# TensorE's order of scores, weighted sums and work-bank tasks in a fused attention kernel

## The chip, the core and the metric

The kernel runs on one core of a Trainium2 chip. The metric is the device time of one execution in microseconds (us); before the change it is 2196.08 us, the median of three runs (2194.22 to 2198.04).

## What is computed

The input x has 16 sequences of 512 tokens with 256 channels. An attention layer with two sets of keys and values comes first, then a gated recurrence over the 16 sequences as steps. The attention part, which the change concerns, is per sequence:

```python
q = heads(x @ Wq)                                   # 16 heads of 16 channels
out_short = softmax(q @ k_s.T / 4 + decay_bias) @ v_s   # decay_bias[i, j] = -|i - j| * (1 - decay)
out_long  = softmax(q @ k_l.T / 4) @ v_l
out = (alpha * out_short + (1 - alpha) * out_long) @ Wo
x = layernorm(x + out)
```

Behind it, for the recurrence: c = f * c + i * g with three gates from x and c, h = tanh(x Wo' + c Uo' + b), and a second layernorm(x + h).

## The kernel before, in words

**Units and slots.** For every sequence b (a batch) there are UNITS = 8 units. A unit is four heads of one of the two attentions: even units are the long one, odd ones the short one with its bias. A unit has TC = 4 slots, one for each chunk of 128 keys, so a batch has 32 slots. Scores are computed twice. `scores(b, s, hp)` makes them with the keys on the partitions, for the exponential (kind "b" below), and `scores_for_max(b, s, hp)` with the queries on the partitions, for the row maxima of the unit that is AHEAD = 8 slots further (kind "a"). Each call makes two heads (hp is 0 or 1), one in each half of the array's rows, and fills one pair of PSUM banks with 128 x 1024 numbers. In odd units `bias` and `bias_for_max` add small bf16 products on the diagonal blocks (`diagonals`) and only then is the pair full.

**Three pairs of banks.** The 16 fills of a unit go round PAIRS = 3 pairs of banks in the order of the list FILLS (line 107). `banks_free` (line 605) makes TensorE wait for the reader of the fill three places earlier in that list: ScalarE's exponential for a "b" fill, VectorE's reduction for an "a" fill. In this text b11 means kind "b", slot 1 of the unit, hp 1, and so on.

**The other work on TensorE.** `weigh_before` (line 673) is the weighted sum of the slot before, probabilities by values, in eight matmuls of 32 columns each side by side; it waits for both exponentials of that slot. `work_task` (line 718) is one task of the list TASKS in a single work bank: "kq" projects keys or queries of the next batch, in two halves, "v" projects values, "ot" turns the attention output, "wo" is the output projection, and "turn" (slot 1 of every unit) turns the unit's weighted sums and the next unit's maxima. `work_free` waits until the readers of the task before are done. A turn waits for ScalarE's copy of the weighted sums (`pv_copied`).

**The readers.** Each engine runs its own program in the order written. VectorE, per slot (lines 553 to 583): the reduction of hp 0, in slot 0 also of hp 1, then its part of the slot's task ("kq": the rest of the split into two parts in `rest`, L517; "ot": likewise; "turn": L526, L532 and L536; "wo": `add_rows`, L547 and L551), then in slots 1 to 3 the reduction of hp 1. ScalarE, per slot (lines 417 to 447): the exponential of hp 0 (L392), its part of the task (a copy, L403, L407 or L415), the exponential of hp 1, and in slot 0 of a unit the copy of the weighted sums of the unit before (L447). SyncE loads the keys, queries and the row of maxima for the units ahead. GpSimd does small sums.

The order on TensorE is written out by hand in `body`, for four slots. A stretch of scores below is a run of score calls with neither weighted sum nor task between. Before, a unit has seven: b00 a00; b01 a01; a10 b10 b11; b20 a11 a20; b21 a21; b30 a30; b31 a31.

Of the kernel before, what the change touches and what calls it, by code (L numbers as in the profile page):

```python
# [21 lines left out]
TC = L // P  # L22
# [44 lines left out]
def exists(b):  # L67

    return not isinstance(b, int) or 0 <= b < B
# [24 lines left out]
def has_task(b, s):  # L94
# [5 lines left out]
    if kind == "kq" and b == -1 and KQ_ORDER.index(n[0]) < EARLY:  # L100
# [3 lines left out]

FILLS = [("b", 0, 0), ("a", 0, 0), ("b", 0, 1), ("a", 0, 1), ("a", 1, 0), ("b", 1, 0), ("b", 1, 1), ("b", 2, 0),
         ("a", 1, 1), ("a", 2, 0), ("b", 2, 1), ("a", 2, 1), ("b", 3, 0), ("a", 3, 0), ("b", 3, 1), ("a", 3, 1)]


def fill_of(b, s, which, hp):
# [26 lines left out]
def attention_phase(nc, shared, x, xT, x1, Wq, Wks, Wkl, Wo, mix, decay, wx, uc, gate_bias, wo, uo, bo, in_c, ident, tri, eye, qrows, krows, kab):  # L138
    ctx = ExitStack()
    with ctx:  # L140
# [215 lines left out]
        def _(act):  # L356
# [38 lines left out]
            def part_or_values(b, s):  # L395

                if not has_task(b, s):
                    return
                kind, n, off = TASKS[s]
                bb = b + off  # L400
                if kind == "ot":
                    wait(act, full["ot"], bb, 2, n + 1)
                    act.activation(ot_h[:, n, :], work[:, :], ACT.Copy).then_inc(ot_hi, 1)  # L403
                if kind == "kq" and n[1]:
                    m = n[0]
                    wait(act, full["kq"], bb, 6, KQ_ORDER.index(m) + 1)
                    act.activation(kq_h[:, m % 3, m // 3, :], work[:, :], ACT.Copy, scale=SCALE if m % 3 == 1 else 1.0).then_inc(kq_hi, 1)  # L407
                if kind == "v":
                    wait(act, full["v"], bb, 8, n[-1] + 1)
                    if n[0] == 4:  # L410
                        wait(act, pv_full, bb, SLOTS, 0)
                    for m in n:
                        src = work[:, H * (m % 2):H * (m % 2) + H].rearrange("p (a h d) -> p a h d", a=2, d=HD)
                        dst = vals[:, m % 4, m // 4, :, 0:8 * VW].rearrange("p a (h e) -> p a h e", e=VW)[:, :, :, 0:HD]
                        act.activation(dst, src, ACT.Copy).then_inc(done["v"], 1)  # L415

            def body(b):
                for s in range(SLOTS):
                    if s == XT_SLOT and b >= 0 and exists(b + 1):
                        wait(act, x_loaded, b + 1, 16, 16)  # L420
                        act.activation(xt_h[(b + 1) % 2][:, :, :], xt_in, ACT.Copy).then_inc(xt_hi, 1)
                    if s == XT_LOAD_SLOT and exists(b + 1) and exists(b + 2):
                        wait(act, xt_hi, b + 1, 1, 1)
                        wait(act, xt_lo, b + 1, 1, 1)
                        act.dma_start(xt_in, xT[b + 2].rearrange("(k p) n -> p k n", p=P)).then_inc(x_loaded, 16)
                    if s == 21 and exists(b):
                        wait(act, done["wo"], b, 4, 0)
                        act.dma_start(x_res[:, :, :], x[b].rearrange("(t p) n -> p t n", p=P)).then_inc(res_loaded, 16)
                    if exists(b):
                        exp_pair(b, s, 0)  # L430
                    part_or_values(b, s)
                    if exists(b):
                        exp_pair(b, s, 1)
                    if 0 <= s - NORM_SLOT < TC and exists(b - 1):
                        t = s - NORM_SLOT
                        wait(act, ln_step, b - 1, 4, 3 + 4)
                        act.activation(res[:, t, :], res[:, t, :], ACT.Identity, bias=nmr[:, t:t + 1],
                                       scale=rstd[:, t:t + 1]).then_inc(normed, 1)
                        if t == TC - 1:
                            wait(act, normed, b - 1, TC, TC)  # L440
                            act.dma_start(x1[b - 1].rearrange("(t p) n -> p t n", p=P), res[:, :, :]).then_inc(x1_stored, 16)
                    if s % 4 == 0:

                        bb, u = (b, s // 4 - 1) if s else (b - 1, UNITS - 1)
                        if exists(bb):
                            wait(act, pv_full, bb, SLOTS, 4 * u + 4)
                            act.activation(pv_sb[:, u % 2, :], pv_ps[:, :], ACT.Copy).then_inc(pv_copied, 1)  # L447
# [4 lines left out]
        def _(dve):  # L452
# [100 lines left out]
            def body(b):  # L553
                for s in range(SLOTS):
                    if s == 22 and exists(b - 1):
                        wait(dve, bn_done, b - 1, TC, TC)
                    bb, u = unit_of(b, (s + AHEAD) // 4)
                    def reduce(hp, bb=bb, u=u, s=s):
                        if exists(bb):
                            wait(dve, a_full, bb, 8 * UNITS, 8 * u + 2 * (s % 4) + hp + 1)  # L560
                            dve.reduce_max(maxes[:, u % 2, :, hp, s % 4], pairs_ps[pair_of(b, s, "a", hp)][:, :, :],  # L561
                                           mybir.AxisListType.X).then_inc(a_reduced, 1)

                    reduce(0)
                    if s % TC == 0:
                        reduce(1)
                    if has_task(b, s):
                        kind, n, off = TASKS[s]
                        if kind == "kq" and n[1]:
                            m = n[0]  # L570
                            rest(kq_l[:, m % 3, m // 3, :], kq_h[:, m % 3, m // 3, :], kq_hi, kind, b + off, KQ_ORDER.index(m),
                                 SCALE if m % 3 == 1 else 1.0)
                        if kind == "ot":
                            rest(ot_l[:, n, :], ot_h[:, n, :], ot_hi, kind, b + off, n, 1.0)
                        if kind == "turn":
                            turn(b, n)
                        if kind == "wo":
                            add_rows(b + off, *n)
                    if s % TC:
                        reduce(1)  # L580
                    if s == 22 and exists(b - 1):
                        for t in range(TC):
                            dve.bn_aggr(mv[:, t, :], stats[:, t, :]).then_inc(mv_done, 1)
# [4 lines left out]
        def _(pe):  # L588
# [79 lines left out]
            def bias_for_max(b, s, hp):  # L668

                if s // 4 % 2 and exists(unit_of(b, (s + AHEAD) // 4)[0]):  # L670
                    diagonals(pairs_ps[pair_of(b, s, "a", hp)], 0, s % 4).then_inc(a_full, 1)
# [90 lines left out]

            def body(b):
                for s in range(0, SLOTS, TC):
                    scores(b, s, 0)
                    scores_for_max(b, s, 0)
                    bias(b, s, 0)
                    bias_for_max(b, s, 0)
                    work_task(b, s)
                    scores(b, s, 1)  # L770
                    scores_for_max(b, s, 1)
                    bias(b, s, 1)
                    bias_for_max(b, s, 1)
                    weigh_before(b, s)
                    scores_for_max(b, s + 1, 0)
                    scores(b, s + 1, 0)
                    bias_for_max(b, s + 1, 0)
                    bias(b, s + 1, 0)
                    scores(b, s + 1, 1)
                    bias(b, s + 1, 1)  # L780
                    work_task(b, s + 1)
                    weigh_before(b, s + 1)
                    scores(b, s + 2, 0)
                    scores_for_max(b, s + 1, 1)
                    bias(b, s + 2, 0)
                    bias_for_max(b, s + 1, 1)
                    scores_for_max(b, s + 2, 0)
                    bias_for_max(b, s + 2, 0)
                    work_task(b, s + 2)
                    scores(b, s + 2, 1)  # L790
                    scores_for_max(b, s + 2, 1)
                    bias(b, s + 2, 1)
                    bias_for_max(b, s + 2, 1)
                    weigh_before(b, s + 2)
                    scores(b, s + 3, 0)
                    scores_for_max(b, s + 3, 0)
                    bias(b, s + 3, 0)
                    bias_for_max(b, s + 3, 0)
                    work_task(b, s + 3)
                    scores(b, s + 3, 1)  # L800
                    scores_for_max(b, s + 3, 1)
                    bias(b, s + 3, 1)
                    bias_for_max(b, s + 3, 1)
                    weigh_before(b, s + 3)

            pe.wait_ge(xt_lo, 1)
# [501 lines left out]
```

## Time and profile before

| | |
|---|---|
| time, median of three runs | 2196.08 us |
| the profiled execution's own time | 2197.7 us |
| its span | 2195.9 us |
| TensorE matmuls busy | 2108.2 us (96%) |
| weight loads busy | 1142.5 us (52%) |
| VectorE busy | 1632.4 us (74%) |
| ScalarE busy | 1469.5 us (67%) |
| GpSimd busy | 134.6 us (6%) |
| mean granted clock of TensorE | 0.983 of full speed |

The span goes from the first to the last instruction. Busy time of matmuls is made with modelled ends, so the distance from one start to the next tells more than a duration. The attention phase fills about the first 1750 us, the recurrence the rest. A row of the order of time has the start in us from the span's start, the duration in us, the engine (PE is TensorE's matmul, PEld its weight load, DVE VectorE, ACT ScalarE), the line of the kernel, the operation, output<-input, and the count of merged instructions; an idle time before it stands in brackets with what ended it. On TensorE, L626 is `scores` (kind b), L652 `scores_for_max` (kind a), L602 the diagonals, L690 the weighted sum, L594 a projection, L756 and L760 the turn.

### The profile page before, as it was taken

Reading aid. Unit: us, or ns where it says so; the run is one execution under the profiler, and the core shown is the slowest. Engines: PE = TensorE matmul, PEld = TensorE weight load, DVE = VectorE, ACT = ScalarE, POOL = GpSimd, SP = SyncE. Lnnn points to the kernel's source line nnn. Section 1 sums busy time; section 2 is a strip of 40 time slices with the busy share of each in tenths; the row PEclk is TensorE's granted clock in tenths of the full one; section 3 lists DMA queues with packets and bytes.
Section 4 is the critical chain, followed back from the end, with each engine's and each line's share of the span. In section 5 each row is a group of like instructions: output and inputs, shape, how many; then the busy total and the mean of one; then the engine's idle time right before and its main releaser. Section 6 shows DMA issues by size and latency. Waiting matters only on the chain.

```text
span 2195.9 us, 41695 instructions
## 1 busy us (share of the span) xinstructions
PE 2108.2 (96%) x16608; PEld 1142.5 (52%) x16608; DVE 1632.4 (74%) x2094; ACT 1469.5 (67%) x1762; POOL 134.6 (6%) x186
## 2 busy tenths in 40 slices
PE   6999999999999999999999999999999869999995
PEld 3444444444444444444444444444444338888873
DVE  6888888888888888888888888888888723333347
ACT  2777777777777777777777877777777643233338
POOL 0000000000000000000000000000000000000005
PEclk8999999999999999999999999999999969999998
DMA  4222222222222222222222222222222130000007
GB/s 109 57 57 55 67 54 64 56 65 57 65 56 64 55 64 61 57 64 55 64 54 64 54 64 55 64 58 64 57 55 55 33 118 29 29 19 29 29 10 258
DMA packets 91251, 134.14 MB, mean 61 GB/s; under 512 B 21300, under 2 KB 43572, under 8 KB 91076
## 3 DMA queue, kind: packets, MB, share of 16 engines
q1 hardware_dynamic: 66948, 97.91, 17.9%
q10 hardware_dynamic: 24128, 33.79, 4.8%
q8 instruction: 122, 2.00, 0.4%
q14 instruction: 53, 0.43, 0.1%
HBM read 37.77 MB, written 16.78 MB: 25 GB/s over the span
## 4 chain that ended last, share of the span: by engine, by line
PE 89%; ACT 4%; DVE 3%; issue 2%; DMA 1%; POOL 1%; ACTq 0%; SPq 0%; DVEq 0%; POOLq 0%
PE pv_ps L690 21%; PE pair_ps L626 17%; PE work L594 15%; PE pair_ps L652 12%; PE banks L1160 12%; PE work L756 3%; PE pair_ps L602 3%; ACT probs L392 2%; PE banks L1153 2%; DVE maxes L561 1%; ACT summed L1014 1%; PE banks L1201 1%; PE banks L1144 1%; PE work L760 1%; DVE res L547 1%
## 5 line engine op out<-in xcount | busy, mean ns | idle before, releaser
L561 DVE TENSOR_REDUCE maxes<-pair_ps 128x2 f32<-128x1024 f32 x1024 | 1227.8, 1221 | 240.0 <-PE pair_ps L602 154.7
L392 ACT ACTIVATE probs<-pair_ps,small 128x1024 f32<-128x1024 f32 x512 | 563.2, 1113 | 230.2 <-PE pair_ps L602 228.8
L392 ACT ACTIVATE probs<-pair_ps 128x1024 f32<-128x1024 f32 x512 | 516.5, 1023 | 159.7 <-PE pair_ps L626 154.6
L690 PE MATMUL pv_ps<-probs,vals 128*32 128x512 f32 x4096 | 549.0, 608 | 0.0
L626 PE MATMUL pair_ps<-q_op,k_op 56*128 56x512 f32 (+1 forms) x2048 | 480.2, 478 | 13.9 <-ACT probs L392 10.7
L652 PE MATMUL pair_ps<-k_op,q_op 55*128 55x512 f32 x2048 | 434.5, 432 | 7.3 <-ACT probs L392 4.5
L626 PEld LDWEIGHTS pair_ps<-q_op,k_op 56*128 56x128 f32 (+1 forms) x2048 | 192.2, 184 | 446.1 <-DVE maxes L561 205.6
L652 PEld LDWEIGHTS pair_ps<-k_op,q_op 55*128 55x128 f32 x2048 | 195.7, 186 | 151.7 <-issue 107.3
L602 PE MATMUL pair_ps<-eye_b,tri_b 64*128 64x64 bf16 x4096 | 163.7, 194 | 0.0
L602 PEld LDWEIGHTS pair_ps<-eye_b,tri_b 64*128 64x128 bf16 x4096 | 94.3, 96 | 115.1 <-issue 93.4
L690 PEld LDWEIGHTS pv_ps<-probs,vals 128*32 128x32 f32 x4096 | 80.8, 108 | 97.5 <-issue 87.7
L333 POOL TENSOR_TENSOR o_sum<-o_att 128x512 f32<-128x512 f32 x32 | 41.1, 1285 | 1283.5 <-DVE o_att L536 1283.5
L948 ACT ACTIVATE act_out<-banks,bias 128x512 f32<-128x512 f32 x96 | 65.3, 687 | 73.6 <-PE banks L1160 73.6
L1037 DVE TENSOR_TENSOR xs_l<-banks,xs_h 128x512 fp32r<-128x512 f32 x32 | 20.6, 684 | 104.1 <-ACT xs_h L957 104.1
L957 ACT ACTIVATE xs_h<-banks 128x512 fp32r<-128x512 f32 x32 | 17.4, 596 | 115.0 <-PE banks L1144 111.6
L756 PE MATMUL work<-ident_sb,pv_sb 128*128 128x128 f32 x512 | 83.6, 286 | 10.9 <-ACT pv_sb L447 10.2
L594 PE MATMUL work<-xt_h,w_hi 128*128 128x512 f32 x184 | 92.4, 502 | 0.0
L447 ACT ACTIVATE pv_sb<-pv_ps 128x512 f32<-128x512 f32 x128 | 76.6, 598 | 22.5 <-PE pv_ps L690 15.5
L594 PE MATMUL work<-wv_hi,xt_h 128*128 128x256 f32 x256 | 84.3, 329 | 4.5 <-DVE w_lo L498 3.4
L517 DVE SCALAR_TENSOR_TENSOR kq_l<-work,kq_h 128x512 fp32r<-128x512 f32 x92 | 63.6, 691 | 29.2 <-ACT kq_h L407 29.2
L1160 PE MATMUL banks<-s_h,uc_h 128*128 128x512 f32 x192 | 76.0, 396 | 0.0
L1045 DVE SCALAR_TENSOR_TENSOR keep<-act_out,state 128x512 f32<-128x512 f32 x32 | 22.0, 688 | 71.9 <-ACT act_out L948 71.9
(147 smaller groups left out, 2507.5 us busy)
## 6 DMA issues: line engine op xcount, KB each, us to landing
k_op<-kq_h SPq DMA_DIRECT2D x508, 64.0 KB, 2.2
q_op<-kq_h SPq DMA_DIRECT2D x256, 64.0 KB, 2.2
k_op<-kq_l SPq DMA_DIRECT2D x254, 64.0 KB, 2.3
x_step<-in_xT ACTq DMA_DIRECT2D x16, 512.0 KB, 4.0
q_op<-kq_l SPq DMA_DIRECT2D x128, 64.0 KB, 2.2
x_res<-in_x ACTq DMA_DIRECT2D x16, 512.0 KB, 3.9
x_dram<-res ACTq DMA_DIRECT2D x16, 512.0 KB, 2.9
x_back<-x_dram SPq DMA_DIRECT2D x16, 512.0 KB, 5.4
```

Of the source, the lines that this page charges most:

```text
L392: act.activation(probs[:, s % 2, 2 * hp:2 * hp + 2, :], pairs_ps[pair_of(b, s, "b", hp)][:, :, :], ACT.Exp, scale=LAM if s // 4 % 2 else 1 ...
L447: act.activation(pv_sb[:, u % 2, :], pv_ps[:, :], ACT.Copy).then_inc(pv_copied, 1)
L517: dve.scalar_tensor_tensor(dst, work[:, :], scale, hi.bitcast(F32), ALU.mult, ALU.subtract).then_inc(done[kind], 1)
L561: dve.reduce_max(maxes[:, u % 2, :, hp, s % 4], pairs_ps[pair_of(b, s, "a", hp)][:, :, :], mybir.AxisListType.X).then_inc(a_reduced, 1)
L594: last = pe.matmul(out, lhs(a, k), rhs(c, k), start=(k == 0 and a + c == 0), stop=(k == KC - 1 and c == 1))
L602: yield pe.matmul(bank[:, P * chunk + HALF * half:P * chunk + HALF * half + HALF], tri_b[at:at + HALF, which, half, :], eye_b[at:at + HALF ...
L626: last = pe.matmul(banks[:, j, :], k[HALF * j:HALF * j + rows, hp, P * c:P * c + P], q[HALF * j:HALF * j + rows, hp, :], start=True, stop= ...
L652: last = pe.matmul(banks[:, j, :], q[at:at + MAX_ROW, hp, P * c:P * c + P], k[at:at + MAX_ROW, hp, :], start=True, stop=u % 2 == 0)
L690: last = pe.matmul(pv_ps[32 * h:32 * h + 32, :], vals[:, c, g // 2, att, at:at + 32], probs[:, s % 2, h, :], start=(c == 0), stop=(c == TC ...
L756: last = pe.transpose(work[:, P * t:P * t + P], pv_sb[:, sums[1] % 2, P * t:P * t + P], id_sb[:, :])
L948: act.activation(act_out[:, k, g, :], gate_ps[n], ACT.Tanh, bias=bias[:, g, k:k + 1], scale=0.5 if g < 2 else 1.0).then_inc(gate_done, 1)
L1160: last = pe.matmul(gate_ps[n], lhs[a][:, g, k, P * mc:P * mc + P], rhs[d][:, k, :], start=start and m == 0, stop=stop and m == len(parts) - 1)
```

## The change

TensorE's order in a unit is written anew, and FILLS with it. Stretches of scores become six: a00 b00 a01; b01 a10; b10 a11 b11; b20 a20 a21; b21 a30; b30 a31 b31. In slots 1 and 2 the weighted sum stands directly ahead of the work-bank task. On VectorE the reduction of hp 1 stands ahead of the task in slots 0 to 2, and behind it only in slot 3. On ScalarE the slot's task stands ahead of the first exponential in slot 3. No operation is added or removed.

```diff
-FILLS = [("b", 0, 0), ("a", 0, 0), ("b", 0, 1), ("a", 0, 1), ("a", 1, 0), ("b", 1, 0), ("b", 1, 1), ("b", 2, 0),
-         ("a", 1, 1), ("a", 2, 0), ("b", 2, 1), ("a", 2, 1), ("b", 3, 0), ("a", 3, 0), ("b", 3, 1), ("a", 3, 1)]
+FILLS = [("a", 0, 0), ("b", 0, 0), ("a", 0, 1), ("b", 0, 1), ("a", 1, 0), ("b", 1, 0), ("a", 1, 1), ("b", 1, 1),
+         ("b", 2, 0), ("a", 2, 0), ("a", 2, 1), ("b", 2, 1), ("a", 3, 0), ("b", 3, 0), ("a", 3, 1), ("b", 3, 1)]
...
+                    if s % TC == TC - 1:
+                        part_or_values(b, s)
                     if exists(b):
                         exp_pair(b, s, 0)
-                    part_or_values(b, s)
+                    if s % TC < TC - 1:
+                        part_or_values(b, s)
...
                     reduce(0)
-                    if s % TC == 0:
+                    if s % TC < TC - 1:
                         reduce(1)
...
-                    if s % TC:
+                    if s % TC == TC - 1:
                         reduce(1)
...
                 for s in range(0, SLOTS, TC):
+                    scores_for_max(b, s, 0)
                     scores(b, s, 0)
-                    scores_for_max(b, s, 0)
+                    bias_for_max(b, s, 0)
                     bias(b, s, 0)
-                    bias_for_max(b, s, 0)
+                    scores_for_max(b, s, 1)
+                    bias_for_max(b, s, 1)
                     work_task(b, s)
                     scores(b, s, 1)
-                    scores_for_max(b, s, 1)
+                    scores_for_max(b, s + 1, 0)
                     bias(b, s, 1)
-                    bias_for_max(b, s, 1)
+                    bias_for_max(b, s + 1, 0)
                     weigh_before(b, s)
-                    scores_for_max(b, s + 1, 0)
                     scores(b, s + 1, 0)
-                    bias_for_max(b, s + 1, 0)
+                    scores_for_max(b, s + 1, 1)
                     bias(b, s + 1, 0)
+                    bias_for_max(b, s + 1, 1)
                     scores(b, s + 1, 1)
                     bias(b, s + 1, 1)
+                    weigh_before(b, s + 1)
                     work_task(b, s + 1)
-                    weigh_before(b, s + 1)
                     scores(b, s + 2, 0)
-                    scores_for_max(b, s + 1, 1)
+                    scores_for_max(b, s + 2, 0)
                     bias(b, s + 2, 0)
-                    bias_for_max(b, s + 1, 1)
-                    scores_for_max(b, s + 2, 0)
                     bias_for_max(b, s + 2, 0)
+                    scores_for_max(b, s + 2, 1)
+                    bias_for_max(b, s + 2, 1)
+                    weigh_before(b, s + 2)
                     work_task(b, s + 2)
                     scores(b, s + 2, 1)
-                    scores_for_max(b, s + 2, 1)
+                    scores_for_max(b, s + 3, 0)
                     bias(b, s + 2, 1)
-                    bias_for_max(b, s + 2, 1)
-                    weigh_before(b, s + 2)
-                    scores(b, s + 3, 0)
-                    scores_for_max(b, s + 3, 0)
-                    bias(b, s + 3, 0)
                     bias_for_max(b, s + 3, 0)
                     work_task(b, s + 3)
+                    scores(b, s + 3, 0)
+                    scores_for_max(b, s + 3, 1)
+                    bias(b, s + 3, 0)
+                    bias_for_max(b, s + 3, 1)
                     scores(b, s + 3, 1)
-                    scores_for_max(b, s + 3, 1)
                     bias(b, s + 3, 1)
-                    bias_for_max(b, s + 3, 1)
                     weigh_before(b, s + 3)
```

## Rows read from the trace of the kernel before

**Rows 1.** Busy time in one stretch: us, busy us of each engine (instructions), clock, DMA

```profile
146.74:1661.83 1515.09, 1501.09 (x12939) 723.06 (x12936) 1269.57 (x1499) 1139.52 (x1303) 91.68 (x98) 1.00 0.24 60
```

**Rows 2.** Order of time on TensorE: the same turn, one batch apart

```profile
1012.50 0.27 PE L760 MATMUL work<-ident_sb,maxes 128*16 128x128 f32 x1
...
1120.70 0.27 PE L760 MATMUL work<-ident_sb,maxes 128*16 128x128 f32 x1
```

**Rows 3.** Order of time on TensorE in an even unit; last line: the next even one

```profile
1048.23 0.39 PE L594 MATMUL work<-w_hi,ot_h 128*128 128x256 f32 x1
...
1049.14 0.50 PE L626 MATMUL pair_ps<-q_op,k_op 56*128 56x512 f32 x2
...
1049.80 1.06 PE L690 MATMUL pv_ps<-probs,vals 128*32 128x512 f32 x8
1050.80 0.50 PE L652 MATMUL pair_ps<-k_op,q_op 55*128 55x512 f32 x2
...
1053.38 0.50 PE L626 MATMUL pair_ps<-q_op,k_op 56*128 56x512 f32 x2
1053.72 0.64 PE L652 MATMUL pair_ps<-k_op,q_op 55*128 55x512 f32 x4
1054.29 0.50 PE L594 MATMUL work<-xt_h,w_hi 128*128 128x512 f32 x1
...
1056.86 0.50 PE L626 MATMUL pair_ps<-q_op,k_op 56*128 56x512 f32 x2
...
1058.41 0.50 PE L626 MATMUL pair_ps<-q_op,k_op 56*128 56x512 f32 x2
...
1080.90 0.50 PE L626 MATMUL pair_ps<-q_op,k_op 56*128 56x512 f32 x2 [0.15 <-DVE maxes L561]
```

**Rows 4.** Order of time on TensorE in an odd unit

```profile
1066.54 0.49 PE L626 MATMUL pair_ps<-q_op,k_op 57*128 57x512 f32 x2
...
1067.24 0.48 PE L652 MATMUL pair_ps<-k_op,q_op 55*128 55x512 f32 x2
...
1067.73 0.50 PE L594 MATMUL work<-xt_h,w_hi 128*128 128x512 f32 x1
...
1068.62 0.49 PE L626 MATMUL pair_ps<-q_op,k_op 57*128 57x512 f32 x2
...
1069.40 1.06 PE L690 MATMUL pv_ps<-probs,vals 128*32 128x512 f32 x8
```

**Rows 5.** Order of time of the weight loads in the even unit

```profile
1052.38 0.16 PEld L690 LDWEIGHTS pv_ps<-probs,vals 128*32 128x32 f32 x8 [0.22 <-issue]
...
1053.49 0.19 PEld L652 LDWEIGHTS pair_ps<-k_op,q_op 55*128 55x128 f32 x2
```

**Rows 6.** Waits on TensorE in the fourteen batches: us in total, times, longest

```profile
PE work L756 <- ACT pv_sb L447: 8.7, 14, 0.6
```

**Rows 7.** Order of time on VectorE in even units

```profile
1049.91 1.23 DVE L561 TENSOR_REDUCE maxes<-pair_ps 128x2 f32<-128x1024 f32 x1 [0.35 <-PE pair_ps L652]
1051.05 0.41 DVE L547 TENSOR_TENSOR res<-work,x_res 128x256 f32<-128x256 f32 x1
...
1051.84 1.21 DVE L561 TENSOR_REDUCE maxes<-pair_ps 128x2 f32<-128x1024 f32 x1
...
1059.76 1.21 DVE L561 TENSOR_REDUCE maxes<-pair_ps 128x2 f32<-128x1024 f32 x1
...
1079.64 1.21 DVE L561 TENSOR_REDUCE maxes<-pair_ps 128x2 f32<-128x1024 f32 x1
```

**Rows 8.** Order of time on ScalarE: odd unit, even unit, odd unit

```profile
1011.78 2.11 ACT L392 ACTIVATE probs<-pair_ps,small 128x1024 f32<-128x1024 f32 x2
...
1057.40 1.02 ACT L392 ACTIVATE probs<-pair_ps 128x1024 f32<-128x1024 f32 x1 [0.65 <-PE pair_ps L626]
1058.52 0.60 ACT L407 ACTIVATE kq_h<-work 128x512 fp32r<-128x512 f32 x1
...
1067.39 1.11 ACT L392 ACTIVATE probs<-pair_ps,small 128x1024 f32<-128x1024 f32 x1 [0.71 <-PE pair_ps L602]
```

## The prediction

> **What bounds the kernel now.** I read the share of busy time first, over fourteen batches in the steady part of the attention phase: TensorE is busy 1501.09 of 1515.09 us, VectorE 1269.57, ScalarE 1139.52 [rows 1]. The reader should see that only 14.00 us, 1.0 us a batch, is bare idle on TensorE, and that VectorE has 16% to spare on average. Then the period: the turning of the maxima in one unit and the same a batch later start 1012.50 and 1120.70, so a batch takes 108.20 us, eight units of about 13.5 us, [rows 2]. Sixteen batches make some 1731 us of the span of 2195.9; the rest is set-up and the recurrence, which the change doesn't touch. Then the order of work inside a unit, by the start times on TensorE [rows 3, 4], because a matmul's end is modelled and its start is not. I price everything from start to start.
>
> **Boundaries, the gain.** A stretch of scores is a run of pairs of banks with nothing else between. Without diagonals (even units) a stretch of two pairs takes 1049.80 - 1049.14 = 0.66 us and one of three 1054.29 - 1053.38 = 0.91 [rows 3]. The third pair adds less than the half of 0.66, since the first pair of a stretch is 0.34 long (1053.38 to 1053.72), and of the 0.57 left the middle one has about 0.24, the last, up to the next kind of work, 0.33. Before, a unit has five stretches of two and two of three: 5 x 0.66 + 2 x 0.91 = 5.12. After, two of two and four of three: 1.32 + 3.64 = 4.96. To three digits I take 0.18 us. With diagonals (odd units) two pairs take 1069.40 - 1068.62 = 0.78 and three 1067.73 - 1066.54 = 1.19 [rows 4]: 5 x 0.78 + 2 x 1.19 = 6.28 before, 2 x 0.78 + 4 x 1.19 = 6.32 after, nothing gained: the third pair comes behind eight small matmuls and pays its entry again. So 4 x 0.18 = 0.7 us a batch.
>
> The trace overlaps a following pair's weight load with the matmul before it: the load of 1053.49 starts 0.11 us into the matmuls that began at 1053.38, on the same two halves of the array's rows [rows 3, 5]. The Trainium skill ("TensorE: Matmul & The Clock Gate", section "The mechanism") says that a weight load overlaps running matmuls only when the row group differs. By that rule a longer stretch would hide no load, and of the 0.7 us only what is not the load's would be left, an estimated 0.3, which moves the result by 6 us; the rows differ from the page here, and I go by the rows.
>
> The weighted sum directly ahead of a work-bank task (twice a unit) has no row in the steady part. The nearest is the other way round, turn to weighted sum: its weights are not loaded ahead, since the load at 1052.38 comes after 0.22 us in which nothing is loaded [rows 5]. One bound is a full boundary, as everywhere; the other that load and leaving (0.10 + 0.09) are both free at 16 places a batch, 3.0 us. I take the full boundary, nearest to that row.
>
> **Waits that go.** The turn waits for the copy of the weighted sums, 8.7 us in 14 batches [rows 6]; with a weighted sum (1.00 us) put ahead of it, this 0.6 us a batch is covered. Other waits of today: the second block of slot 2 in one unit waits for a reduction (0.15 idle at 1080.90 [rows 3]), and several pairs start 0.1 late. Idle alone bounds all of them from below at 1.0 us a batch; my sum of the pieces of a batch (4 x 5.12 + 4 x 6.28 of scores, 32 weighted sums at 1.00, an estimated 28 of work-bank tasks) gives 105.6, so 2.6 from above. I take 2.0 as gone. SyncE's loads and the row of maxima keep their count and their queue order, with about a unit of lead; their price is zero, and would be the load's landing time if a unit's lead were lost. ScalarE's own move (slot 3's task ahead of its first exponential) follows the new order on TensorE and holds nothing back; without it the copy would wait one exponential.
>
> **Waits that come, the loss.** In the new filling order each fill waits for whoever reads the fill three places earlier. Write a10 for the block for the maximum of slot 1, pair 0, and b11 for the scores of slot 1, pair 1. Now b11 takes a10's banks; before it took a01's, and a10's went to b20, a weighted sum and a turn later. VectorE still reads a10 behind the task of slot 0. Walk the third unit (even, output projection with its add and statistics), from the start of a00:
>
> TensorE comes to b11 after three pairs 0.91, the task 1049.14 - 1048.23 = 0.91, two pairs 0.66, the weighted sum 1050.80 - 1049.80 = 1.00, and two pairs of its stretch 0.57: 4.05 us [rows 3]. VectorE can start a00 at 0.54 (a first pair of a stretch at 1056.86, its reader at 1057.40 [rows 3, 8]), is free for the next 1.14 later (1049.91 to 1051.05), reaches a10 1.93 after a01 (1049.91 to 1051.84: reduction, add, statistics) and needs 1.21 for it [rows 7]; the release reaches TensorE 0.05 later (1079.64 + 1.21 = 1080.85 against 1080.90 [rows 3, 7]). That is 0.54 + 1.14 + 1.93 + 1.21 + 0.05 = 4.87. TensorE waits 0.82, and 0.10 more since the weights are then not loaded ahead (0.34 against 0.24): **0.92 us**. The units with the other such tasks (first: turned output; fifth: two chunks) shift both sides by like amounts, and I price them the same. Queued behind this wait on TensorE are a weighted sum and the turn, for which VectorE then waits in turn: it can't use the time.
>
> The fourth unit (odd, the same task): b11 is due at 1.19 + 0.91 + 0.78 + 1.00 + 0.70 = 4.58; a00 is ready at 1067.39 - 1066.54 = 0.85 [rows 4, 8], a10 is released at 0.85 + 1.14 + 1.93 + 1.21 + 0.05 = 5.18.
>
> At each unit's start b00 now takes the banks of a31, the last block that VectorE reads, behind the rest of the key or query projection. After the slot-3 task: the copy starts 1058.52 - 1058.41 = 0.11 later, lasts 0.60, the rest of the projection ends its turn on VectorE 0.64 after that (1059.76 - 1059.12), then 1.21 of reduction and 0.05 [rows 3, 7, 8]: 2.61. TensorE is there after three pairs, a weighted sum and a00: 0.91 + 1.00 + 0.34 = 2.25. It waits 0.36 + 0.10 = **0.46 us** where the unit before is even and has a projection (into the fourth, sixth and eighth). In the fourth this delays b11 and a00's diagonals alike, so it adds: 0.60 + 0.10 + 0.46 = 1.16. Into even units the exponentials are late instead: two of them (2.11 in a row, so 1.00 apart and 1.11 long) and the release take 0.85 + 1.00 + 1.11 + 0.05 = 3.01 from b30 [rows 4, 8] against 1.19 + 1.00 + 0.57 = 2.76 for a01: 0.25 + 0.10 = 0.35. In the first, third and fifth this is swallowed by the wait for b11 except for 0.1.
>
> **The sum.** New waits a batch: first, third and fifth unit 3 x 1.02 = 3.1; fourth 1.2; sixth and eighth 0.9; seventh 0.35; second some 0.1: 5.6. With 0.7 and 2.0 off, +2.9 us a batch. It holds for fifteen batches; the first has no output tasks in its early units and comes out near zero. 15 x 2.9 = 43 us, on the profiled execution's 2197.7 us (span 2195.9) gives 2241, on the median of 2196.1, which is 1.6 lower, **2239 us**. Bounds: only the b11 waits come (3 x 0.92 + 0.70 = 3.5) and 2.6 goes: +0.2 a batch, 2199; waits of 6.5 (ScalarE's normalisations delay the copy in the seventh unit as well), 0.5 gained and only 1.0 gone: +5.0, 2271.
>
> **The rivals.**
> *Not slower: VectorE keeps up.* If a10 were released before 4.05 in the units with a task, the new order would simply be shorter: 0.7 + 2.0 off in sixteen batches, 2153 us. For it: 16% spare on VectorE [rows 1], and 1.14 less is needed in units whose slot-0 task has no VectorE part. Against: the 4.87, of which no term can shrink. It decides at 0.82 us less on VectorE between a00 and a10. Chance 0.10.
> *Only the b11 waits.* The projections' rest and the exponentials keep up at the unit's start, as the long wait for b11 puts TensorE later against its readers: 3.5 - 2.7 = +0.8 a batch, 2208 us. Chance 0.15.
> *A free step from weighted sum to task.* 3.0 us a batch back: +2.9 - 3.0 = -0.1, about 2195 us, the change's own reason undone or paid for. The other way's row speaks against it. Chance 0.07.
> The Trainium skill ("TensorEngine Tiling (Array Packing)", section "Key Properties") says that changing the tiling mode drains TensorE; weighted sum and task are of different modes, so by that rule this rival falls. No run here shows this step.
> *VectorE sets the pace throughout.* A late reader passes its delay to the next unit: +5.0, 2271 us. Its work is 8 x 1.14 + 0.64 + 0.79 and an estimated 1 for the turn, 11.6 of 13.5 us a unit, which speaks against. Chance 0.08.
>
> **How the numbers follow.** The forecast has 0.60, and its own range is 2215 to 2262. The range of 2194 to 2264 takes in the second and third rivals too, and leaves out the first and the last. A measurement tells 0.2% (4.4 us) from no change: faster 0.12 (the first rival and part of the third), same 0.06 (the rest of the third and the edge of the second), slower 0.82.
>
> **What would show it.** In the trace after: a wait of 0.8 us on TensorE for the maxima in the middle of the third stretch, in the first, third, fourth and fifth unit of a batch and not in the others; one of some 0.4 for b00 into the fourth, sixth and eighth; no wait of the turn for its copy; a period of 111.1 us instead of 108.2; three-pair stretches of 0.91 and 1.19. I am wrong if the third stretch runs through in the third unit, or if a task behind a weighted sum starts without its boundary.

## The result

The changed kernel takes 2268.62 us (2267.54 to 2269.57, four runs) against 2195.54, also the median of four runs: 1.0328 times the time before, with a 95% interval of 1.0314 to 1.0342. It is 73 us slower. The prediction had 2239 us, so its sign was right, its mechanism was there, and its size was too small: 43 us where 73 came. The time lies outside the range of 2194 to 2264.

| | before | after |
|---|---|---|
| span of the profiled execution | 2195.9 us | 2266.5 us |
| one batch, turn to turn | 108.20 us | 112.93 us |
| TensorE matmuls busy | 2108.2 us (96%) | 2136.8 us (94%) |
| VectorE busy | 1632.4 us (74%) | 1627.0 us (72%) |
| ScalarE busy | 1469.5 us (67%) | 1456.7 us (64%) |
| mean granted clock | 0.983 | 0.982 |

The busy time of fourteen batches answers to [rows 1]: us, then the busy us of TensorE's matmuls, weight loads, VectorE, ScalarE and GpSimd.

```profile
155.34:1736.56 1581.22, 1526.68 (x12939) 723.19 (x12936) 1265.06 (x1498) 1127.95 (x1303) 91.52 (x98) 1.00 0.23 57
```

The same 12939 matmuls are spread over 1581.22 us instead of 1515.09, and the bare idle of TensorE grew from 14.00 to 54.54 us. VectorE and ScalarE do as much as before. The granted clock is 1.00, full speed, in both. Of the 70.6 us that the span grew, these fourteen batches have 66.1 and the first batch has 7.2 (its first unit, from turn to turn, takes 16.89 us instead of 12.50). 1.4 us come ahead of the first batch, and what lies behind the fourteen is 4.1 shorter. That 4.1 can't be put down to the order: from the last turn to the end, the traces of all the kernels here take anything from 434 to 442 us.

The turn of one unit a batch apart in the changed kernel, for [rows 2]:

```profile
946.03 0.27 PE L763 MATMUL work<-ident_sb,maxes 128*16 128x128 f32 x1
...
1058.96 0.27 PE L763 MATMUL work<-ident_sb,maxes 128*16 128x128 f32 x1
```

And TensorE's waits in the fourteen batches, for [rows 6]: us in total, times, longest.

```profile
PE pair_ps L629 <- DVE maxes L564: 35.2, 98, 0.4
PE work L597 <- DVE ot_l L520: 8.6, 14, 0.6
PE pv_ps L693 <- ACT pv_sb L450: 8.6, 14, 0.6
```

There are 98 waits for the maxima, seven a batch, and I had forecast seven: b11 in four units, b00 in three. The other two kinds come once a batch each, and I had neither. The turn's wait for its copy (8.7 us) has not gone. It stands as 8.6 us ahead of a weighted sum.

**The third unit as walked.** TensorE's order of time, for [rows 3]:

```profile
980.71 0.50 PE L655 MATMUL pair_ps<-k_op,q_op 55*128 55x512 f32 x2
981.05 0.39 PE L629 MATMUL pair_ps<-q_op,k_op 56*128 56x512 f32 x2
981.56 0.49 PE L655 MATMUL pair_ps<-k_op,q_op 55*128 55x512 f32 x2
981.98 0.39 PE L597 MATMUL work<-w_hi,ot_h 128*128 128x256 f32 x1
...
984.55 0.50 PE L629 MATMUL pair_ps<-q_op,k_op 56*128 56x512 f32 x2
984.89 0.40 PE L655 MATMUL pair_ps<-k_op,q_op 55*128 55x512 f32 x2
985.58 0.49 PE L629 MATMUL pair_ps<-q_op,k_op 56*128 56x512 f32 x2 [0.30 <-DVE maxes L564]
986.01 0.64 PE L693 MATMUL pv_ps<-probs,vals 128*32 128x512 f32 x4
```

b11 starts 985.58 - 980.71 = 4.87 us after a00, which is the walk's 4.87. The idle in brackets says 0.30, since a matmul's modelled end hides part of it; the steps from start to start say 0.69 for a11 to b11 where a stretch without a wait has 0.24, and 0.43 for b11 where it has 0.33. The first stretch takes 981.98 - 980.71 = 1.27 instead of 0.91: the 0.36 into an even unit, where 0.35 was forecast. VectorE in the same unit, for [rows 7]:

```profile
981.25 2.36 DVE L564 TENSOR_REDUCE maxes<-pair_ps 128x2 f32<-128x1024 f32 x2 [0.59 <-PE pair_ps L655]
983.53 0.42 DVE L550 TENSOR_TENSOR res<-work,x_res 128x256 f32<-128x256 f32 x1
983.98 0.43 DVE L554 BATCH_NORM_STATS2 stats<-res 128x6 f32<-128x256 f32 x1
984.32 2.34 DVE L564 TENSOR_REDUCE maxes<-pair_ps 128x2 f32<-128x1024 f32 x2
```

The last row's first reduction is a10's. It starts at 984.32, behind add and statistics, and b11 stands until 985.58.

### The profile page after: what moved, and what is told of

Read it like the earlier page. It is cut to its first block, busy times and chain, and to the rows that moved or that the text cites. A ratio compares the mean times of both kernels' runs of the same rounds, so it can differ in the third digit from the quotient of the medians.

```text
span 2266.5 us, 41695 instructions
## 1 busy us (share of the span) xinstructions
PE 2136.8 (94%) x16608; PEld 1143.7 (50%) x16608; DVE 1627.0 (72%) x2094; ACT 1456.7 (64%) x1762; POOL 133.7 (6%) x186
## 4 chain that ended last, share of the span: by engine, by line
PE 74%; DVE 16%; ACT 6%; issue 2%; DMA 1%; POOL 1%; ACTq 0%; SPq 0%; DVEq 0%; POOLq 0%
PE pv_ps L693 17%; PE pair_ps L629 13%; PE work L597 13%; PE banks L1163 12%; DVE maxes L564 11%; PE pair_ps L655 9%; PE work L759 3%; PE pair_ps L605 3%; PE banks L1156 2%; ACT probs L392 2%; DVE kq_l L520 1%; ACT kq_h L407 1%; DVE stats L554 1%; DVE res L550 1%; ACT summed L1017 1%
## 5 line engine op out<-in xcount | busy, mean ns | idle before, releaser
L392 ACT ACTIVATE probs<-pair_ps,small 128x1024 f32<-128x1024 f32 x512 | 556.8, 1114 | 235.8 <-PE pair_ps L605 228.3
L629 PE MATMUL pair_ps<-q_op,k_op 56*128 56x512 f32 (+1 forms) x2048 | 500.9, 485 | 44.5 <-DVE maxes L564 44.3
L605 PE MATMUL pair_ps<-eye_b,tri_b 64*128 64x64 bf16 x4096 | 177.0, 194 | 0.0
L605 PEld LDWEIGHTS pair_ps<-eye_b,tri_b 64*128 64x128 bf16 x4096 | 100.3, 96 | 121.8 <-issue 93.0
L529 DVE TENSOR_SCALAR shift_rows<-work 16x128 fp32r<-16x128 f32 x128 | 35.7, 279 | 139.9 <-PE work L763 139.9
L693 PEld LDWEIGHTS pv_ps<-probs,vals 128*32 128x32 f32 x4096 | 81.2, 108 | 105.1 <-issue 87.9
L759 PEld LDWEIGHTS work<-ident_sb,pv_sb 128*128 128x128 f32 x512 | 53.9, 141 | 108.2 <-issue 106.5
L415 ACT ACTIVATE vals<-work 128x256 f32<-128x256 f32 x128 | 47.8, 387 | 58.7 <-PE work L597 57.0
```

What stands on the lines that cost most here:

```text
L392: act.activation(probs[:, s % 2, 2 * hp:2 * hp + 2, :], pairs_ps[pair_of(b, s, "b", hp)][:, :, :], ACT.Exp, scale=LAM if s // 4 % 2 else 1 ...
L605: yield pe.matmul(bank[:, P * chunk + HALF * half:P * chunk + HALF * half + HALF], tri_b[at:at + HALF, which, half, :], eye_b[at:at + HALF ...
L629: last = pe.matmul(banks[:, j, :], k[HALF * j:HALF * j + rows, hp, P * c:P * c + P], q[HALF * j:HALF * j + rows, hp, :], start=True, stop= ...
L693: last = pe.matmul(pv_ps[32 * h:32 * h + 32, :], vals[:, c, g // 2, att, at:at + 32], probs[:, s % 2, h, :], start=(c == 0), stop=(c == TC ...
L759: last = pe.transpose(work[:, P * t:P * t + P], pv_sb[:, sums[1] % 2, P * t:P * t + P], id_sb[:, :])
```

## The two waits that were missed

**The work bank in the second unit.** TensorE:

```profile
976.14 0.50 PE L629 MATMUL pair_ps<-q_op,k_op 57*128 57x512 f32 x2
...
977.62 0.39 PE L597 MATMUL work<-wv_hi,xt_h 128*128 128x256 f32 x1 [0.61 <-DVE ot_l L520]
```

ScalarE, then VectorE, in the same stretch:

```profile
976.25 0.60 ACT L403 ACTIVATE ot_h<-work 128x512 fp32r<-128x512 f32 x1 [0.91 <-PE work L746]
...
976.88 0.69 DVE L520 SCALAR_TENSOR_TENSOR ot_l<-work,ot_h 128x512 fp32r<-128x512 f32 x1 [0.22 <-ACT ot_h L403]
```

The turned output of slot 6 keeps the bank from 976.14, the task's end, until 976.88 + 0.69 = 977.57. Between the tasks of slots 2 and 3 TensorE has only one stretch of two pairs now, 0.80 us. Before, it had two such stretches and a weighted sum. The next task starts at 977.62, so it waits 0.68. I had followed the banks of the scores round the new order, but not the work bank.

**The copy in the eighth unit.** TensorE, then ScalarE:

```profile
1055.60 0.50 PE L629 MATMUL pair_ps<-q_op,k_op 57*128 57x512 f32 x2
...
1056.63 0.23 PE L605 MATMUL pair_ps<-eye_b,tri_b 64*128 64x64 bf16 x4
1057.47 1.06 PE L693 MATMUL pv_ps<-probs,vals 128*32 128x512 f32 x8 [0.61 <-ACT pv_sb L450]
```

```profile
1055.67 0.59 ACT L440 ACTIVATE res<-res,nmr,rstd 128x256 f32<-128x256 f32 x1
...
1056.73 0.60 ACT L450 ACTIVATE pv_sb<-pv_ps 128x512 f32<-128x512 f32 x1 [0.47 <-ACT res L440]
```

I had written that a weighted sum put ahead of the turn covers the turn's wait. But that weighted sum starts a new accumulation in the bank that the copy reads, so it waits for the same copy (`pv_copied` in `weigh`). The wait moved one place up and kept its size.

## Experiments

The kernel before was timed again beside each group of runs: 2197.2 us beside a10_first, a31_first, copy_first and tasks_swapped, 2196.3 beside all_four, before_copy_first and old_readers, 2195.7 beside the two with more statistics, and 2197.5 beside the two with a normalisation in slot 29. A period below is the time of one batch from turn to turn, as a mean of the fourteen batches.

### The task ahead of a10, undone: a10_first

```diff
-                    reduce(0)
+                    if s % TC != 1:
+                        reduce(0)
                     if s % TC < TC - 1:
                         reduce(1)
+                    if s % TC == 0:
+                        reduce(0, s=s + 1)
```

> The changed kernel, with one edit on VectorE: the reduction of a10 stands ahead of the task of slot 0 and not behind it. Its work stays the same. Theory of the chain (b11 waits because a10 is read behind that task): the waits in the middle of the third stretch in the first, third, fourth and fifth unit (0.68, 0.56, 0.57 and 0.68 us in the changed kernel's trace) go, 2.5 us a batch, 37 us in fifteen batches: 2268.6 - 37 = 2231 us. Rival (VectorE has too much to do in those units): the wait moves to the task's readers or to b20, and the time stays within 8 us of 2268. Rival (the step from weighted sum to task costs more than a boundary): the time doesn't move either.

Measured: 2232.94 us (2230.17 to 2234.5), 1.0162 times before (1.0145 to 1.0179). The step is -36 us where 37 was expected. In the unit with the output projection the third stretch now runs through:

```profile
828.77 0.50 PE L632 MATMUL pair_ps<-q_op,k_op 56*128 56x512 f32 x2
829.11 0.40 PE L658 MATMUL pair_ps<-k_op,q_op 55*128 55x512 f32 x2
829.35 0.46 PE L632 MATMUL pair_ps<-q_op,k_op 56*128 56x512 f32 x2
829.74 0.64 PE L696 MATMUL pv_ps<-probs,vals 128*32 128x512 f32 x4
```

b11 follows a11 after 0.24. TensorE's waits in fourteen batches are these:

```profile
PE pair_ps L632 <- DVE maxes L564: 14.1, 42, 0.5
PE work L600 <- DVE ot_l L520: 8.7, 14, 0.6
```

There are 42 for the maxima, three a batch, where the changed kernel has 98. VectorE's work is the same, so half of the 73 us come from the place of one reduction in each unit.

### More work on VectorE, in two places: extra_slot0 and extra_slot2

The second kernel has `s % TC == 2` in this place. The results of the added instruction are used by nothing.

```diff
+                    if s % TC == 0:
+                        dve.bn_stats(extra[:, s // TC, :], tri_sb[:, 0, :, :].rearrange("p a n -> p (a n)"))
                     if has_task(b, s):
```

> The changed kernel, with one statistics instruction of 256 columns more on VectorE in every unit (0.34 us behind another, its result unused), put in slot 0 between the reduction of a01 and the task, so ahead of a10's. Theory of the chain: every such us ahead of a10 is a us of waiting for b11 in the four units that wait there, 4 x 0.34 = 1.4 us a batch, and up to 0.3 in the others: 2268.6 + 15 x 1.4 to 1.7 = 2290 to 2294 us. Rival (VectorE's load as such): the same as the run with the instruction in slot 2.

> The changed kernel, with the same eight statistics instructions a batch on VectorE, put in slot 2 behind the reductions of a20 and a21, where VectorE then waits for a30's banks. Theory of the chain: it falls into that wait but for some 0.1 us in the four even units: 2268.6 + 15 x 0 to 0.5 = 2269 to 2276 us. Rival (VectorE's load as such): 2290 us, as in slot 0.

Measured: 2289.28 us (2286.05 to 2294.19) with it in slot 0, 2275.55 (2274.62 to 2276.83) in slot 2. By the traces a batch grew by 1.17 us in the first case and by 0.05 in the second. Of the 8.1 us between the span of the second and that of the changed kernel only 0.6 lie in the fourteen batches; 1.7 lie ahead of the first batch, 3.4 in the last and 2.5 behind it, and what made them there is not shown. In the first case the first, third and fourth units grew by 0.30 to 0.35 each; the fifth grew by only 0.08. There VectorE stands at the add until TensorE's double task is done, and the statistics fell into that pause: a point that my forecast of 4 x 0.34 had missed. So the rival, VectorE's load as such, has fallen: the same instruction costs next to nothing where VectorE waits and nearly its full length where it stands ahead of a10.

### b00 and the projection's rest: a31_first

```diff
-                    if s % TC < TC - 1:
-                        reduce(1)
+                    reduce(1)
...
-                    if s % TC == TC - 1:
-                        reduce(1)
```

> The changed kernel, with one edit on VectorE: in slot 3 the reduction of a31 stands ahead of the rest of the key or query projection. Theory of the chain (b00 takes a31's banks): the waits at the start of the fourth, sixth and eighth unit (0.54, 0.54 and 0.6 us in the changed kernel's trace) go, and those into even units stay, since they hang on the exponentials: 1.7 us a batch, 25 us: 2244 us. Rival (VectorE has too much to do): the projection's rest is now late for the next task in the work bank, or the reductions of the next unit are, and the time stays within 8 us of 2268.

Measured: 2241.87 us (2241.71 to 2243.71), 1.0202 times before (1.0185 to 1.0219): -27 us for 25 expected. The period fell by 1.72 us, and 56 waits for the maxima are left, the four of b11 in each batch.

### The copy ahead of the normalisation: copy_first, and the same in the kernel before

```diff
-                    if 0 <= s - NORM_SLOT < TC and exists(b - 1):
-                        ...
                     if s % 4 == 0:
                         ...
+                    if 0 <= s - NORM_SLOT < TC and exists(b - 1):
+                        ...
```

> The changed kernel, with one edit on ScalarE: in slot 28 the copy of the weighted sums stands ahead of a row's normalisation and not behind it. Theory of the chain (the weighted sum of a unit's first slot overwrites the bank that the copy reads, so the wait that I thought covered is only moved from the turn to it): the wait of 0.7 us ahead of that weighted sum in the eighth unit goes, 15 x 0.7 = 10 us: 2258 us. Rival (that weighted sum waits for its own exponentials): no change, 2268 us.

> The kernel before, with one edit on ScalarE: in slot 28 the copy of the weighted sums stands ahead of the row's normalisation. It tells whether the wait of 0.6 us a batch, for which the turn waits in the kernel before, is the same one: then it goes too, 15 x 0.6 = 9 us, 2187 us. If the turn waits for something else that ends at the same time, the time stays at 2196 us.

Measured: 2263.01 us (2260.64 to 2266.61) and 2191.73 us (2188.43 to 2193.61, 0.9981 of before, 0.9972 to 0.9990). In both kernels the unit that held the wait got shorter, by 0.70 and 0.65 us, and the next span from turn to turn longer, by 0.34 and 0.37. It is one wait, moved by the change. Half of the gain was given back, though. My reason for that is that the normalisation and the start of its store now stood ahead of slot 29's exponentials, which read the next banks; it is put to the test under before_norm29.

### The work bank's tasks swapped: tasks_swapped

```diff
-TASKS = {... 6: ("ot", 1, -1), 7: ("v", (7,), 0), ...
+TASKS = {... 6: ("v", (7,), 0), 7: ("ot", 1, -1), ...
```

> The changed kernel, with the tasks of slots 6 and 7 swapped: a value projection in slot 6 and the turned attention output in slot 7. Theory of the chain (slots 2 and 3 have only one stretch of two pairs between their tasks, 0.79 us, while the turned output keeps the work bank for 1.47 us of copy and rest): the wait of 0.68 us for the work bank in the second unit goes, and the rest in slot 7 costs next to nothing at the start of the third: 15 x 0.65 = 10 us, 2259 us. Rival (VectorE is late there because it now does both reductions of the slot first): the wait goes with the rest of the output to the third unit's start, 2268 us.

Measured: 2264.1 us (2263.14 to 2266.97), -4.5 us for 9.6 expected; the period fell by 0.31, not by 0.65. The wait for the work bank is gone, but the shorter task in slot 7 brings TensorE to the last stretch earlier, and there a31 stands for the banks of b21:

```profile
750.86 0.51 PE L629 MATMUL pair_ps<-q_op,k_op 57*128 57x512 f32 x2
751.50 0.50 PE L655 MATMUL pair_ps<-k_op,q_op 55*128 55x512 f32 x2
```

ScalarE read b21 from 750.33 to 751.44:

```profile
750.33 1.11 ACT L392 ACTIVATE probs<-pair_ps,small 128x1024 f32<-128x1024 f32 x1 [0.36 <-PE pair_ps L605]
```

0.64 us from the first pair to the second instead of 0.34. The chain was right and its successor was missed.

### All four edits together: all_four

> The changed kernel with all four edits: a10 ahead of slot 0's task, a31 ahead of slot 3's, the copy ahead of the normalisation, tasks of slots 6 and 7 swapped. TensorE's order is that of the change. Theory of the chain: 2.5 + 1.7 + 0.7 + 0.7 = 5.6 us a batch off, a period of 107.4 us where the kernel before has 108.2: 2268.6 - 83 = 2186 us, some 10 us under the kernel before. What is left are the waits of 0.37 us into even units and pairs that start 0.1 late. Rival (VectorE has too much to do): the edits don't add up, and it stays above the kernel before. Rival (TensorE's own boundaries cost more in the new order): the period stays above 108.2 even with the waits gone.

Measured: 2197.51 us (2196.09 to 2201.05), 1.0010 times before (1.0000 to 1.0019). The four periods fell by 2.38, 1.72, 0.37 and 0.31, in sum 4.78 us, and together by 4.64: the waits are nearly separate and add up. The 2186 us expected were too low mainly by the halves of the last two. Some 3.3 us of waits a batch are left (an estimate from the starts on TensorE, worked out as told under "Boundaries" below), and the largest part, 1.5, is the exponentials into the even units, one of four places a batch:

```profile
837.56 0.50 PE L655 MATMUL pair_ps<-k_op,q_op 55*128 55x512 f32 x2
837.90 0.39 PE L629 MATMUL pair_ps<-q_op,k_op 56*128 56x512 f32 x2
838.40 0.49 PE L655 MATMUL pair_ps<-k_op,q_op 55*128 55x512 f32 x2
```

a01 comes 0.50 after b00 instead of 0.24. By the same estimate the kernel before has 2.3 us of waits a batch, so the new order still waits 1.0 us longer, and that takes up the 0.8 which its boundaries save. The second rival (dearer boundaries) falls although the period stayed at 108.3: the work without waits is 105.1 us a batch here and 105.9 before.

### A normalisation in slot 29: before_norm29 and all_four_norm29

```diff
-NORM_SLOT = 25
+NORM_SLOTS = (25, 26, 27, 29)
...
```

The first run is the kernel before with this edit, the second is all_four with it.

> The kernel before, with one edit on ScalarE: the fourth of the row normalisations stands in slot 29, where ScalarE has no task, and not in slot 28 ahead of the copy. With the copy put first in slot 28 the eighth unit got 0.65 us shorter in the trace and the next unit 0.37 longer. Theory: the normalisation and its store then stood ahead of slot 29's exponentials, whose banks TensorE needs; from slot 29's end it delays less, and more of the 0.65 is kept: a period of 107.6 to 107.9 us, 2186 to 2190 us. Rival (the 0.37 comes from TensorE being 0.65 us earlier against all its readers, wherever the normalisation stands): 108.0, 2192 us as with the copy first.

> The kernel with all four edits and the changed order on TensorE, where the fourth normalisation also goes to slot 29. Its trace has 0.3 us of waiting in the eighth unit's fourth stretch, where slot 29's exponentials are read behind the normalisation. Theory of the chain: up to 0.3 us a batch off, a period of 108.0 to 108.2 us, 2193 to 2197 us, so the changed order with its waits mended still doesn't beat the kernel before with the same ScalarE edit. Rival: no change, 2197.5 us.

Measured: 2187.38 us (2185.71 to 2189.59), 0.9956 times before (0.9942 to 0.9970), and 2194.8 us (2193.03 to 2196.61), 0.9988 (0.9979 to 0.9997). The first beats both kernels by an edit of ScalarE's order alone. With the same edit the changed order, its waits mended, is still 7 us behind the old one. But in the steady part the two are nearly level: a batch takes 107.77 us in before_norm29 and 107.89 in all_four_norm29. Of the 9.1 us between their spans, 7.5 lie ahead of the fourteen batches, 4.0 of them in the first unit (16.51 us from turn to turn where the old order has 12.50).

The runs also test the reason given for the half that the copy's move gave back. In the changed order the span behind the eighth unit's turn fell from 13.59 (all_four) to 13.25 us, and it is 13.24 in a10_first, where the copy is not moved. So there the normalisation's place was the whole of it. In the old order it is 13.20 in the kernel before, 13.56 with the copy first and 13.45 with the normalisation in slot 29 as well: only 0.11 of the 0.36 came back. The rest fits the rival of before_norm29 (TensorE is simply earlier against all its readers), but no run shows it.

### The old order of the readers: old_readers

The diffs of VectorE and ScalarE are taken back, TensorE's stays.

> The changed kernel's order on TensorE and of the fills, with the orders of VectorE and ScalarE of the kernel before: the readers' part of the change is undone. Theory of the chain: a20 takes a11's banks, and a11 is now read behind the turn, so every unit waits some 1.9 us more at the fourth stretch, and the projection's copy behind an exponential adds 1.2 us in six units: 22 us a batch, 2500 to 2600 us. Rival (the readers' order matters little, VectorE's load sets the time): 2268 us within 20.

Measured: 2901.26 us (one run). The waits for a11's reduction are as expected, 1.86 us longer than a pair's step (start to start 2.20 instead of 0.34):

```profile
1013.94 0.50 PE L626 MATMUL pair_ps<-q_op,k_op 56*128 56x512 f32 x2
1016.14 0.73 PE L652 MATMUL pair_ps<-k_op,q_op 55*128 55x512 f32 x4 [1.70 <-DVE maxes L561]
```

But the time is 300 us over the forecast, and the clock has a part in it. In three windows of 100 us (us, busy us of the engines, then the clock in the third column from the right):

```profile
1000.00:1100.00 100.00, 83.29 (x576) 38.42 (x572) 58.15 (x72) 48.85 (x55) 2.86 (x5) 0.85 0.17 42
1100.00:1200.00 100.00, 83.29 (x635) 38.10 (x634) 60.86 (x70) 55.06 (x64) 3.65 (x2) 0.90 0.18 44
1200.00:1300.00 100.00, 84.47 (x555) 39.84 (x556) 55.34 (x67) 50.85 (x61) 4.12 (x6) 0.81 0.17 41
```

The fourteen batches of this trace tell the two apart:

```profile
192.52:2343.23 2150.71, 1793.06 (x12939) 832.94 (x12936) 1267.34 (x1498) 1128.54 (x1303) 91.09 (x98) 0.87 0.17 42
```

The bare idle of TensorE is 357.65 us against 54.54 in the changed kernel, 21.7 more a batch, where 22 were forecast in sum. The same 12939 matmuls are busy for 1793.06 us instead of 1526.68, 19.0 more a batch, at a clock of 0.87 instead of 1.00. So the forecast of the waits held, and the longer matmuls at the lower clock made up the rest: an estimated 15 x 19 = 285 of the 300 us.

## Why the prediction was right or wrong, point by point

- **Boundaries, 0.7 us a batch.** Right. The stretches have the forecast lengths where nothing waits: an even one of three pairs 988.60 - 987.70 = 0.90, an odd one 1.19. An estimate from the starts on TensorE agrees: each stretch, weighted sum and task of eleven steady batches is counted at the length that it has where nothing waits (0.67 and 0.90 us for an even stretch of two and of three pairs, 0.80 and 1.19 for an odd one). That gives 105.9 us of work a batch before and 105.1 in the changed kernel, so 0.8 gained. The 0.3 that I had set beside the 0.7, for longer stretches that hide no weight load, did not come. The rows below show the step from weighted sum to task in the changed kernel.

```profile
987.70 0.50 PE L629 MATMUL pair_ps<-q_op,k_op 56*128 56x512 f32 x2
988.04 0.63 PE L655 MATMUL pair_ps<-k_op,q_op 55*128 55x512 f32 x4
988.60 1.07 PE L693 MATMUL pv_ps<-probs,vals 128*32 128x512 f32 x8
989.59 0.50 PE L597 MATMUL work<-xt_h,w_hi 128*128 128x512 f32 x1
989.93 0.40 PE L597 MATMUL work<-xt_h,w_lo 128*128 128x512 f32 x1
990.17 0.40 PE L597 MATMUL work<-xt_l,w_hi 128*128 128x512 f32 x1
```

- **The step from weighted sum to task.** A full boundary, as I took it: the weighted sum keeps its 0.99 and the task's first matmul its 0.34. The third rival falls. The Trainium skill ("TensorEngine Tiling (Array Packing)", section "Key Properties") says that a change of the tiling mode drains TensorE. The trace agrees: the first matmul behind the change takes 0.34 where the following one of the same task takes 0.24 (989.93 to 990.17).
- **b11 in four units.** Right in place and size: 4.87 walked, 4.87 in the trace; a10_first took 36 us of it back. The first rival (VectorE keeps up) and the fourth (its load sets the pace) fall with this and with the two runs with more statistics. That the fourth rival's time, 2271 us, lies next to the measured 2268.6 is luck.
- **b00 in the fourth, sixth and eighth unit.** Right in place; 0.46 forecast, 0.54, 0.54 and 0.60 there. a31_first took 27 us back, where 3 x 0.46 x 15 is 21. The second rival, that these waits don't come, falls.
- **Waits that go, 2.0 us.** Here the prediction failed first. The size is near: by the same count the kernel before has 2.3 us of waits a batch (0.68 the turn's for its copy, 0.25 the first pair behind the turned output of slot 6, for an exponential, 0.22 the one at 1080.90, the rest pairs late by under 0.1). But the step "with a weighted sum put ahead of it, this 0.6 us is covered" is wrong. That wait came back as 0.7 us ahead of the weighted sum.
- **Waits that come, 5.6 us.** This is the term that was mis-sized: it measured 7.75 us by the starts on TensorE, the copy's 0.7 included, so 2.1 more. By unit they are 1.05, 0.82, 0.93, 1.23, 1.07, 0.65, 0.40 and 1.60. Two waits that I had put at nothing make 1.4 of the 2.1: the work bank's 0.68 in the second unit, which I never looked for, and the copy's 0.7 in the eighth. Over fifteen batches they are 20 of the 30 us that the forecast is short. The rest is spread: b00 waits 0.54 to 0.60 instead of 0.46, and pairs are late by 0.1 in the last stretch of the fourth, sixth and eighth unit, at a00 of the eighth and, twice, behind the value task of the second. Of these I had only "0.1 in the second unit".
- **The first batch, near zero.** Wrong by 7 us. It has no output tasks, but its first unit waits 1.60 and 1.19 for the maxima, while the granted clock is 0.50 (40 to 60 us; 0.61 there in the kernel before). That unit has 4.4 of the 7 us, and the fourth has 2.1. I had not looked into it.
- **Fifteen batches.** Only the fourteen between the first and the last grew by 4.73 each. The last one grew by 0.1 us up to its last turn (92.31 instead of 92.23). That the span grew by just 15 x 4.73 = 71 us is luck: the first batch's 7 us stand in for a last batch that did not grow, and for 4 us less behind the fourteen.
- The sum: 112.93 - 7.75 leaves 105.2 us of work without waits a batch, beside my 105.6 - 0.7 = 104.9 from the pieces and 105.9 by the count of the kernel before. Written as in the prediction, -0.7 for the boundaries, -2.3 for the waits of before and +7.75 make +4.75; measured 4.73. The three terms are an estimate from the starts and depend by some 0.2 on what is taken for the length of a piece without a wait; only their sum is measured.

## What to carry to other kernels

When an order of work is rewritten by hand, every resource with a reader has to be walked round the new order, also those that the change isn't about: here the work bank and the accumulator's bank, each with its own chain of copy and rest. A wait for a copy isn't covered by moving work ahead of the waiter when that work overwrites what is being copied. And a mean load of 84% on an engine says nothing on whether it is late: one reduction behind the wrong task cost half of the loss, while added work in its pauses cost 0.05 us a batch.

## What the hardware showed that was not expected

The granted clock of TensorE fell in the steady part of the one kernel that has waits of nearly 2 us in every unit. In old_readers it was 0.81 to 0.90 over windows of 100 us, where all other kernels have 1.00, and the same weighted sum took 1036.92 - 1035.50 = 1.42 us instead of 1.00, just behind a stretch with a wait of 1.9:

```profile
1035.50 1.50 PE L690 MATMUL pv_ps<-probs,vals 128*32 128x512 f32 x8
1036.92 0.80 PE L594 MATMUL work<-xt_h,w_hi 128*128 128x512 f32 x1
1037.52 0.63 PE L594 MATMUL work<-xt_h,w_lo 128*128 128x512 f32 x1
```

```profile
1036.92:1038.50 1.58, 1.58 (x7) 0.84 (x3) 0.66 (x1) 0.00 (x0) 0.00 (x0) 0.50 0.00 0
```

The projection's first matmul takes 0.60 there where it takes 0.34 at full speed. The last line gives the granted clock of this stretch: 0.50, the lower of the two levels (1.2 instead of 2.4 GHz). In the changed kernel, with waits of up to 0.7 us, the clock stayed at 1.00 through the fourteen batches.
